# The two f16 halves of b made straight from the turned activations, eight short instructions each, and one pair of halves moved

## The reference

```
xn  = layernorm(x)                                 # per token, no weight
h   = rmsnorm(xn) * qkv_norm_w                     # per token, times a weight per channel
q, k, v = split(h @ ternary(qkv_w).T)              # 16 heads of 64
per chunk of 128 tokens and head, with S carried along the batch:
    o = 64**-0.5 * ((q k^T * decay_mask) v + (q * lam_t) S)
    S = lam_T * S + (k * lam_rev)^T v
out = rmsnorm(rmsnorm(o) * norm_w) * proj_norm_w @ ternary(proj_w).T
g   = silu(xn @ ternary(ffn_weight).T + bias)
result = x + out * g
```

## Time and profile before

| | |
|---|---|
| median of 3 runs | 1433.49 us (1432.68 to 1433.99) |
| the profiled execution: own time, span | 1434.04 us, 1432.3 us |
| VectorE, ScalarE, GpSimd busy | 759.2 us, 380.3 us, 525.6 us |
| DMA | 74.64 MB, 52 GB/s on the mean |

### The profile page before, as it was taken

One profiled execution on the slowest core, in us unless ns is written; L12 is line 12 of the kernel. 1 busy time (PEld: TensorE's weight loads), 2 busy tenths in 40 slices (PEclk: granted clock), 3 DMA queues, 4 the chain that ended last, 5 costly groups with the idle time before them and its releaser, 6 DMA issues.

```text
span 1432.3 us, 26710 instructions
## 1 busy us (share of the span) xinstructions
PE 1388.7 (97%) x11537; PEld 952.6 (67%) x11537; DVE 759.2 (53%) x1071; ACT 380.3 (27%) x556; POOL 525.6 (37%) x492
## 2 busy tenths in 40 slices
PE   5999989999999999999999999999999999999998
PEld 2677667676665757667576666767667576676765
DVE  7884271835529165381735629265281744818324
ACT  6882221222213122131222212122131221212211
POOL 1523242434414352353433424353252423524331
PEclk9999999999999999999999999999999999999999
DMA  9420102002010020101102010020201101020000
GB/s 366 193 89 31 64 5 88 10 30 68 31 63 5 30 67 31 63 5 45 53 30 68 23 67 9 30 67 31 63 5 45 53 30 64 5 80 18 16 16 30
DMA packets 27766, 74.64 MB, mean 52 GB/s; under 512 B 6913, under 2 KB 10753, under 8 KB 27650
## 3 DMA queue, kind: packets, MB, share of 16 engines
q1 hardware_dynamic: 27360, 72.92, 15.1%
q10 hardware_dynamic: 290, 0.02, 0.0%
HBM read 56.12 MB, written 16.81 MB: 51 GB/s over the span
## 4 chain that ended last, share of the span: by engine, by line
PE 77%; DVE 7%; issue 2%; ACT 1%; DVEq 0%; ACTq 0%
PE ring L451 27%; PE ring L566 14%; PE ring L437 11%; PE ring L463 11%; PE att_ps L529 3%; PE att_ps L525 3%; PE att_ps L485 3%; DVE arena L856 2%; DVE b_full L798 2%; PE att_ps L507 2%; DVE b_lo L824 2%; PE ring L493 1%; ACT a_hi L1136 1%; DVE a_lo L812 1%; PE ring L580 0%
## 5 line engine op out<-in xcount | busy, mean ns | idle before, releaser
L451 PE MATMUL ring<-b_lo,qkv_q 128*128 128x256 f16 x2048 | 451.2, 273 | 0.0
L451 PE MATMUL ring<-b_hi,qkv_q 128*128 128x256 f16 x2048 | 451.2, 273 | 0.0
L451 PEld LDWEIGHTS ring<-b_hi,qkv_q 128*128 128x128 fp8e4 x2048 | 201.5, 98 | 27.8
L451 PEld LDWEIGHTS ring<-b_lo,qkv_q 128*128 128x128 fp8e4 x2048 | 200.3, 98 | 28.0
L437 PE MATMUL ring<-ffn_q,a_hi 128*128 128x512 fp8e4 x480 | 184.7, 385 | 10.7 <-DVE gate_even L840 7.5
L463 PE MATMUL ring<-qkv_q,b_hi 128*128 128x512 fp8e4 x512 | 194.2, 379 | 0.0
L463 PE MATMUL ring<-qkv_q,b_lo 128*128 128x512 fp8e4 x512 | 194.0, 379 | 0.0
L566 PE MATMUL ring<-proj_q,o_hi 128*128 128x512 fp8e4 x496 | 188.1, 379 | 3.7 <-DVE o_lo L917 3.7
L566 PE MATMUL ring<-proj_q,o_lo 128*128 128x512 fp8e4 x496 | 188.0, 379 | 0.0
L437 PE MATMUL ring<-ffn_q,a_lo 128*128 128x512 fp8e4 x480 | 184.3, 384 | 0.0
L856 DVE TENSOR_TENSOR arena<-att_ps,mask 128x512 f32<-128x512 f32 x128 | 79.4, 682 | 134.4 <-PE att_ps L485 134.0
(11 more groups left out here) (154 smaller groups left out, 2016.3 us busy)
## 6 DMA issues: line engine op xcount, KB each, us to landing
xt<-in_x SPq DMA_DIRECT2D x32, 512.0 KB, 3.4
out<-xt SPq DMA_DIRECT2D x31, 512.0 KB, 2.6
raw<-in_qkv_w SPq DMA_DIRECT2D x24, 512.0 KB, 15.5
y<-in_x_turned SPq DMA_DIRECT2D x14, 512.0 KB, 4.3
y_odd<-in_x_turned SPq DMA_DIRECT2D x14, 512.0 KB, 5.6
raw<-in_ffn_w SPq DMA_DIRECT2D x8, 512.0 KB, 9.8
norm_rows<-norm_out SPq DMA_DIRECT2D x28, 128.0 KB, 4.1
raw<-in_proj_w SPq DMA_DIRECT2D x6, 512.0 KB, 4.8
```

The costliest lines, as they stand in the source:

```text
L451: ins = pe.matmul(ring[:, b, e * BT:(e + 1) * BT], qkv_q[:, cb, o:o + P], part[:, cb, :], start=(cb == 0 and part is b_hi), stop=(cb == NC ...
```

## The change

From block 2 on `b_full` is no longer made. `high_b` makes `b_hi` with four ScalarE instructions of 128 values that read `y_turned` and take the channel's weight as the scale of the instruction, a pointer to one value a partition. `split_b` makes `b_lo` with four VectorE instructions of 128 values, (y times weight) minus `b_hi`, the weight again by pointer. Both `split_b` of chunk 0 of the next block move from the end of `attention(i, 0)` to `attention(i, 1)`, behind the decayed k and in front of `centre`. In block 1, v's second half of chunk 1 moves from behind the scores of chunk 1 to the end of chunk 0, and the list of ring uses follows. The load of the next turned x waits for `b_lo` in place of `b_full`.

```diff
+        V_EARLY = ((0, 0), (0, 1), (1, 0))
@@ tensor_program, attention
-                if i < 2:
+                if (i, c) in V_EARLY:
                     project_v(i, 1, c)
-                else:
+                elif i > 1:
                     ffn(i, c, 0)
...
-                        if i > 1:
+                        if i > 1 or (i, half) == (1, 1):
                             project_v(i, 1, half)
@@ vector_program, split_a, split_b, attention
-                if i != 1:
+                if i == 0:
                     weigh_b(i, c, half, bank)
...
                 dve.wait_ge(s_bhi, of_half(i, c, half))
+                if i > 1:
+                    for cb in range(hs.start, hs.stop):
+                        ins = dve.scalar_tensor_tensor(out=b_lo[:, cb, ts], in0=y_turned[c][:, cb, :],
+                                                       scalar=cols[:, 0, cb:cb + 1], in1=b_hi[:, cb, ts],
+                                                       op0=ALU.mult, op1=ALU.subtract)
+                    ins.then_inc(s_blo, 1)
+                    return
...
+                if more and i > 0 and c == 1:
+                    split_b(i + 1, 0, 0)
+                    split_b(i + 1, 0, 1)
                 if more and i > 0:
                     centre(i + 1, c)
...
                         if i == 0:
                             take_b(1, 0, half)
+                            split_b(1, 0, half)
                         elif more:
                             split_a(i + 1, 0, half)
-                        if more:
-                            split_b(i + 1, 0, half)
@@ scalar_program, high_b
-                act.wait_ge(s_bf, of_half(i, c, half))
                 if i > 0:
                     act.wait_ge(s_vps, of_half(i - 1, c, 1))
+                if i > 1:
+                    act.wait_ge(s_yn, of_turned(i, c))
+                    for cb in range(hs.start, hs.stop):
+                        ins = act.activation(b_hi[:, cb, ts], y_turned[c][:, cb, :], ACT.Copy,
+                                             scale=cols[:, 0, cb:cb + 1])
+                    ins.then_inc(s_bhi, 1)
+                    return
+                act.wait_ge(s_bf, of_half(i, c, half))
@@ sync_program, load_turned
-                    sync.wait_ge(s_bf, of_half(i - 1, c, 1))
+                    sync.wait_ge(s_blo, of_half(i - 1, c, 1))
```

More of the change, by code:

```diff
@@ L304, in program @@
                     for h in range(HALF):
-                        ring_uses += [("b", 1, 0, h)] * (i == 0) + [("v", i, 1, h)] * (i > 1)
+                        ring_uses += [("b", 1, 0, h)] * (i == 0) + [("v", i, 1, h)] * (i > 1 or (i, h) == (1, 1))
                 else:
```

## The result

| | before | after |
|---|---|---|
| median (six runs each) | 1432.59 us (1432.15 to 1433.99) | 1439.14 us (1437.3 to 1439.79) |
| profiled execution: own time, span | 1434.04, 1432.3 us | 1439.31, 1437.9 us |
| VectorE, ScalarE, GpSimd busy | 759.2, 380.3, 525.6 us | 682.9, 413.3, 509.3 us |

The ratio of the times is 1.0041, with a 95% interval of 1.0028 to 1.0054: slower, by more than the 0.2% line. VectorE does 76 us less work, and the kernel takes 6.5 us more.

The account below looks back on a forecast made before the run. VectorE's chain from ffn_bias to o_lo was taken to bound the kernel, with TensorE 97% busy. Terms 1.5 - 1.4 + 4.6 + 0.1 + 0 = +4.8 us gave 1438.8, 1438.3 as a median; 8 in 10 range 1430.5 to 1443.5.

Parts of the forecast that it names:

- seven middle blocks: Blocks 2, 5, 6, 9, 10, 13, 14: the 1.08 us stall goes, yet the projection starts 0.21 us later each, +1.5 us.
- blocks 4, 8, 12: Blocks that open a batch: projection 0.46 us earlier each, -1.4 us; +0.29 each if GpSimd's sum is not earlier.
- blocks 3, 7, 11: Blocks that close a batch: no relief from chunk 0, projection 1.54 us later each, +4.6 us, the largest term.
- block 1, order: Block 1: v's half fills the 3.19 us wait for the state, and the projection starts earlier, -1.3 us.
- block 1, clock: Block 1: the clock loss, hidden under VectorE's splits before, falls on the projection, about +1.4 us.
- clock elsewhere: Outside block 1: one clock fall before (block 12, 1.7 us) and one after, so 0.
- Price of one short b_lo: VectorE: 350 ns for 128 values with a pointer, 0.27 us each after 80 ns overlap, 2.18 us for eight.
- rival A: Short instructions are cheap, 1.6 to 1.7 us for eight: 6.2 us less, 1432.1 us, not slower; chance 0.16.
- The chain to o_lo binds: Chunk 1: VectorE's chain from ffn_bias to o_lo decides; o_lo has 0.2 us of room against 2.18 added.
- Rival B: The chain to o_lo does not bind and all the backlog comes out as time, 16 us: 1418 us; chance 0.05.
- Rival C: Longer single waits let the clock fall, 1.4 to 1.7 us each; three more give 1443 us; chance 0.13.
- ScalarE, GpSimd, DMA: Costs nothing: perhaps 1.2 us more ScalarE work a chunk; GpSimd's sum and the turned load have room.

Follow-up runs that it names:

- e7_constant: The changed kernel with the constant 1.0 in place of the pointer to the weight in VectorE's short b_lo (another output): 1428.71 us.
- e3_move_alone: The kernel before with only both split_b of the next chunk 0 moved behind chunk 1's decayed k; long instructions and b_full stay: 1429.96 us.
- e1_behind: The changed kernel with both split_b of the next chunk 0 taken out of the chain and put behind o_lo: 1411.79 us.
- e4_fill: The changed kernel with matmuls of constants in front of chunk 0's projection in blocks 1, 3, 7 and 11: 1433.24 us.
- e2_old_place: The changed kernel with the short b_lo of the next chunk 0 back in their old place at the end of chunk 0: 1434.66 us.

## Why the prediction was right

The forecast was 1438.3 us, the measurement 1439.14. The change was forecast as +4.8 us and measured as +6.5: the median of the kernel before came out at 1432.59 us over six executions and not at the 1433.49 of three. The terms, read off as the change in the start of each block's projection between the two traces:

| term | forecast | measured |
|---|---|---|
| seven middle blocks | +0.21 each, +1.5 | +0.09, +0.6 |
| blocks 4, 8, 12 | -0.46, -1.4 | -0.68, -2.0 |
| blocks 3, 7, 11 | +1.54, +4.6 | +1.46, +4.4 |
| block 1, order | -1.3 | -1.73 |
| block 1, clock | +1.4 | +2.7 |
| clock elsewhere | 0 | +3.4 - 1.7 = +1.7 |
| sum | +4.8 | +5.7 (span: +5.6) |

The mechanism was right, and the closeness of the sum is in part luck: the terms without the clock came out 2.1 us lower than forecast, the two of the clock 3.0 us higher, and they nearly cancel.

**Price of one short b_lo:** right, and the step on which the sign hung. 350 ns forecast, 343 measured; 0.27 us from start to start, 2.10 / 8 = 0.26 measured, so the overlap of 80 ns holds for short instructions too. With 282 ns (e7_constant) or with two long ones (e3_move_alone) in the same place the kernel is faster than before. That confirms the mechanism, and it puts rival A and the Trainium skill's 194 ns (VectorE: DVE Perf Modes, "The TRN2 errata") aside: they would have given 1.55 to 1.7 us for eight.

**The chain to o_lo binds:** right. In the middle blocks the projection starts 14.62 us after the first ffn half (636.68 - 622.06), forecast 14.75, before 14.54. The missing 0.08 us of the b_lo make most of the difference. Rival B is what e1_behind is: its forecast of 1418 stood for a chain that does not bind, and taking b_lo off the chain gave 1411.79.

**Blocks that open a batch:** GpSimd's sum was early, as taken; TensorE waits for it nowhere in the trace after, so the lower of the two values was the case. The line of the sum there (-2.3 + 2.18 - 0.16) adds up to -0.28; the forecast -0.46 comes out with the 0.18 us more by which `o_lo` is early in the kernel before (459.74 against 459.98, with 0.06 to start).

**Block 1:** the order brought 0.4 us more than worked out. The term of the clock was mis-sized: I took 1.4 us from the scores in the trace before, and the projection lost 9.79 - 7.08 = 2.7. The failed assumption is that a fall costs the same each time. The length of the wait alone does not set the price: in e3_move_alone, behind the same 3.19 us in front of the same scores, the granted clock was 0.50 over the 6.2 us behind the wait, against 0.57 over 3.5 us in the kernel before. What does set it stays open.

**Clock elsewhere:** this was the weak step. I counted one fall before and one after; there were two, in blocks 7 and 11, of 1.68 us each, and that of block 12 went (its ffn half no longer waits). Rival C named it with 0.13 and was half right. e4_fill shows that the waits cause these falls. In the kernel before, too, the number of falls is not fixed: its mean clock over 44 executions goes from 0.995 to 0.999, so counting one fall for it was already a guess on one trace.

**ScalarE, GpSimd, DMA:** hidden, as said. The short b_hi added 33 us of ScalarE work, and no wait of TensorE is for ScalarE or a transfer from block 2 on.

Not settled: whether the two groups in the changed kernel's times (two near 1437.4, four near 1439.4) are one fall more or less. The distance fits 1.7 us, and the two have a mean granted clock of 0.996 where the four have 0.995, but only one execution has a trace. Also the median of e2_old_place lies 2.4 us above its profiled execution. The clock doesn't account for that: nine of its eleven executions have the mean clock of the profiled one, 0.996, and they go from 1432.07 to 1435.73 us.

## What to carry to other kernels

Before adding instructions to a place where an engine "has room", follow the chain from there to the next thing that TensorE waits for: here VectorE was idle half the time, and one stretch of some 9 us with almost no gap decided. Four pieces of 128 values took 1.05 us from start to start where one instruction of 512 takes 0.60, so pieces belong behind the critical result, and not beside long instructions of GpSimd. Run the alternatives for the place of a step: three places gave 1439, 1435 and 1412 us.

## What the runs showed of the hardware

- A pointer to one value a partition costs VectorE 61 ns an instruction against a constant at 128 values (343 and 282 ns, changed kernel and e7_constant), and 59 ns at 8 values (231 and 172 ns).
- Beside GpSimd's two-input instructions, 128-value instructions of VectorE with two SBUF inputs took 1063 ns on the mean instead of 348, and up to 2516 ns (e2_old_place).
- Waits of TensorE of 1.48 us, also ten times in a kernel, left the clock at 2.4 GHz; of three waits of 2.14 us two brought it to 1.2 GHz, at 1.68 us each; 4.46 us cost 2.7. In e1_behind a wait of 2.37 us did not, in its profiled execution. But in e2_old_place one of 1.62 us in block 1 went with a fall, so the length of a wait alone does not decide. Matmuls of constants in the wait kept it up (e4_fill), so a wait of TensorE can cost more than its own length.
